# Split query and key parts laid out by dimension then head, spilled part by part, and fetched back in wider transfers

## What is computed

```python
q = heads(hidden_states @ Wq.T + bq)
k = heads(hidden_states @ Wk.T + bk)
v = heads(hidden_states @ Wv.T + bv)
...
scores = jnp.einsum('bhqd,bhkd->bhqk', qx, kx) * scale
return jnp.einsum('bhqk,bhkd->bhqd', jax.nn.softmax(scores, axis=-1), vx)
...
x = x + _layernorm(_L0_attn_ref(_layernorm(x, axis=-1), L0_attn_Wq, ...), axis=-1)
x = x + _layernorm(_L0_ffn_ref(_layernorm(x, axis=-1), ...), axis=-1)
```

## Time and profile before

| | us |
|---|---|
| median of 3 runs (lowest, highest) | 1994.57 (1987.76, 1997.65) |
| the profiled execution | 2002.51 |
| its span, first to last instruction | 2000.7 |
| PE busy / DVE busy / ACT busy / POOL busy | 1591.1 / 1223.5 / 928.4 / 707.2 |

### The profile page before, as it was taken

One profiled execution on the slowest core, in us unless ns is written; L12 is line 12 of the kernel. 1 busy time (PEld: TensorE's weight loads), 2 busy tenths in 40 slices (PEclk: granted clock), 3 DMA queues, 4 the chain that ended last, 5 costly groups with the idle time before them and its releaser, 6 DMA issues. The chain is left out here.

```text
span 2000.7 us, 35686 instructions
## 1 busy us (share of the span) xinstructions
PE 1591.1 (80%) x10365; PEld 1075.6 (54%) x10430; DVE 1223.5 (61%) x3633; ACT 928.4 (46%) x1788; POOL 707.2 (35%) x716
## 2 busy tenths in 40 slices
PE   3878888887887887887888887747999999999800
PEld 2534444444444444444444444536888888888700
DVE  6746765765765765765756755333565656565367
ACT  1045655655655655655656657412333333333234
POOL 1011223413413413314324313432445444444457
PEclk9889999999999998999999999978999999999955
DMA  3453256256265355364365351564665665566477
GB/s 118 78 107 83 55 124 134 82 126 144 72 127 118 89 137 112 81 146 105 90 148 101 82 138 66 167 204 104 139 137 97 142 135 113 123 135 119 49 257 253
DMA packets 185576, 241.78 MB, mean 121 GB/s; under 512 B 24584, under 2 KB 156048, under 8 KB 185296
## 3 DMA queue, kind: packets, MB, share of 16 engines
q1 hardware_dynamic: 158544, 203.58, 40.2%
q0 software_dynamic: 26880, 36.33, 10.9%
HBM read 133.40 MB, written 105.91 MB: 120 GB/s over the span
## 5 line engine op out<-in xcount | busy, mean ns | idle before, releaser
L956 ACT ACTIVATE pexp<-scT 128x512 f32<-128x512 f32 x768 | 440.6, 599 | 366.0 <-PE scT L743 323.7
L1126 DVE TENSOR_REDUCE mx<-work 128x1 f32<-128x320 f32 (+2 forms) x1024 | 493.3, 549 | 60.1 <-PE work L723 57.8
L1600 POOL DMA_INDIRECT y_rows<-rows_add,row_of x144 | 227.0, 1576 | 294.6 <-DMA y_rows<-rows_add,row_of 210.0
L723 PE MATMUL work<-w 126*128 126x320 bf16 (+4 forms) x1280 | 268.0, 302 | 60.3 <-DVE mx L1126 26.6
L743 PE MATMUL scT<-w 128*128 128x192 bf16 (+3 forms) x1472 | 258.8, 274 | 62.8 <-ACT pexp L956 56.9
L1632 PE MATMUL h_ps<-inT,w1c 128*128 128x256 f32 x1152 | 262.1, 381 | 2.4 <-DVE inT L1684 2.4
L1645 PE MATMUL o_ps<-w,hT 128*128 x1152 | 260.4, 379 | 0.0
L1632 PEld LDWEIGHTS h_ps<-inT,w1c 128*128 128x128 f32 x1152 | 219.7, 191 | 33.1 <-issue 3.1
L743 PEld LDWEIGHTS scT<-w 128*128 128x128 bf16 x1536 | 125.6, 98 | 205.4 <-ACT pexp L956 141.6
L1575 ACT ACTIVATE rows_add<-rows_out,row_share 128x257 f32<-128x257 f32 x144 | 65.6, 503 | 355.2 <-DVE rows_out L1700 256.5
L1645 PEld LDWEIGHTS o_ps<-w,hT 128*128 128x128 f32 x1152 | 213.4, 190 | 26.1
(11 more groups left out here) (173 smaller groups left out, 2172.2 us busy)
## 6 DMA issues: line engine op xcount, KB each, us to landing
w<-split_spill SPq DMA_DIRECT2D x384, 128.0 KB, 5.9
split_spill<-split SPq DMA_DIRECT2D x64, 384.0 KB, 4.7
rows_in<-z_rows SPq DMA_DIRECT2D x72, 265.0 KB, 4.7
y_rows<-pre SPq DMA_DIRECT2D x16, 514.0 KB, 6.6
y<-y_rows SPq DMA_DIRECT2D x16, 514.0 KB, 6.1
x_rows<-x SPq DMA_DIRECT2D x16, 512.0 KB, 2.7
abel_rows<-pre SPq DMA_DIRECT2D x16, 512.0 KB, 5.5
abel_in<-abel_rows SPq DMA_DIRECT2D x16, 512.0 KB, 4.5
```

The lines of the kernel that those rows point to most:

```text
L723: ins = nc.tensor.matmul(work[t][:, at:at + hi - lo], tile(qst[par][0:K_SCORE, h, :], t), kst[par][0:K_SCORE, h, lo:hi], start=True, stop= ...
L956: nc.scalar.activation(pexp[:, (q * GROUP + n) % NPB, :], scT[n % 2][:, :], ACT.Exp, scale=DH ** -0.5).then_inc(s_exp, 1)
L1126: nc.vector.reduce_max(mx[:, c:c + 1], work[t][:, 0:n], AX_X).then_inc(w_free[t], 1)
L1600: pool.indirect_dma_start(kept.y_rows, bass.IndirectOffsetOnAxis(ap=row_of[n][:, r:r + 1], axis=0), rows_add[n % 2][:, r, :], None, comput ...
```

## The change

Six edits belong together.

- Queries and keys lie by dimension, then head, within a tile: partition d * 8 + h instead of h * 16 + d. The columns of the query and key weights are permuted for that on DVE: they are loaded to a scratch place (`wqk_raw`, in `ctxT`), and two copies (one for each half of the contraction) put them into `wqkv` in the new order, ahead of the mask rows' copies. The biases are permuted by their DMA. PE's first projection waits for the copies (`s_wqk`).
- One constant load becomes two, so DVE and PE wait for seven constants at the start.
- DRAM holds the spilled tile part by part (`[2, 4, 3, 128, 512]`). Put writes 384 pieces of 1 KB instead of 128 of 3 KB.
- In that layout the 8 heads of one dimension of one part are 8 KB in one piece, and the 16 dimensions and following parts come right behind.
- The six pairs stand in another order (`Q_PART`, `K_PART`), and key tiles hold their parts in reverse (`held`), so that pairs 0 to 2 read three consecutive parts, pairs 3 and 4 of the keys two consecutive parts, pairs 3 and 4 of the queries the same part twice.
- Restack issues three transfers (`GROUPS`) of 48, 32 and 16 partitions instead of six of 16. A stack half is complete after 6 transfers instead of 12.

```diff
-Q_PART = [0, 0, 1, 1, 0, 2]
-K_PART = [0, 1, 0, 1, 2, 0]
+Q_PART = [0, 1, 2, 0, 0, 1]
+K_PART = [2, 1, 0, 1, 0, 0]
+GROUPS = [(0, 3), (3, 5), (5, 6)]
...
+def held(m, part):
+
+    return 2 - part if m % 2 else part
...
+        wqk_raw = ctxT[:, 0:KC, :]
...
-        spill = nc.dram_tensor("split_spill", [2, 4, P, 3, S], BF16, kind="Internal").ap()
+        spill = nc.dram_tensor("split_spill", [2, 4, 3, P, S], BF16, kind="Internal").ap()
...
-            sp.dma_start(wqkv[:, :, :], a["wqkvT"].rearrange("(k p) o -> p k o", p=P)).then_inc(s_const, 16)
-            sp.dma_start(bqk_sb[:, :], a["bqk"]).then_inc(s_const, 16)
+            wqkv_rows = a["wqkvT"].rearrange("(k p) o -> p k o", p=P)
+            sp.dma_start(wqk_raw, wqkv_rows[:, :, 0:2 * D]).then_inc(s_const, 16)
+            sp.dma_start(wqkv[:, :, 2 * D:3 * D], wqkv_rows[:, :, 2 * D:3 * D]).then_inc(s_const, 16)
+            sp.dma_start(bqk_sb[:, :], a["bqk"].rearrange("(h d) m -> d h m", d=DH)).then_inc(s_const, 16)
...
-                sp.dma_start(spill[par, m], split[:, m, :, :]).then_inc(s_spill[m], 16)
+                sp.dma_start(spill[par, m].rearrange("s p c -> p s c"), split[:, m, :, :]).then_inc(s_spill[m], 16)
...
-                for g, part in enumerate(parts):
-                    src = spill[par, m].rearrange("(h d) s c -> d h s c", d=DH)[:, :, part, :]
-                    sp.dma_start(st[par][g * DH:(g + 1) * DH, 8 * half:8 * half + 8, :], src)\
+                for lo, hi in GROUPS:
+                    first, n = held(m, parts[lo]), hi - lo
+                    src = spill[par, m].rearrange("s (d h) c -> s d (h c)", d=DH)
+                    if n > 1 and parts[lo] == parts[lo + 1]:
+                        src = src[first:first + 1].broadcast_to([n, DH, 8 * S])
+                    else:
+                        src = src[first:first + n]
+                    sp.dma_start(st[par][lo * DH:hi * DH, 8 * half:8 * half + 8, :], src)\
                       .then_inc(s_stack[half], 16)
...
+            for k in range(KC):
+                nc.vector.tensor_copy(wqkv[:, k, 0:2 * D].rearrange("p (m d h) -> p m d h", m=4, d=DH),
+                                      wqk_raw[:, k, :].rearrange("p (m h d) -> p m d h", m=4, d=DH)).then_inc(s_wqk, 1)
```

More of the change, by code:

```diff
@@ L312, in front @@
         turn = ps("turn", [P, S])
-        spill = nc.dram_tensor("split_spill", [2, 4, P, 3, S], BF16, kind="Internal").ap()
+        spill = nc.dram_tensor("split_spill", [2, 4, 3, P, S], BF16, kind="Internal").ap()
         s_const = sem("s_const")
+        s_wqk = sem("s_wqk")
         g_load = sem("g_load")
@@ L390, in front @@
         g_t = sem("g_t")
-        N_CONST, N_LOAD, N_INIT = 6, 6, 7
+        N_CONST, N_LOAD, N_INIT = 7, 6, 7
         LOADS = len(RUNS) * 16
@@ L695, in project @@
                     pe.wait_ge(s_xnT, (b + 1) * KC)
+                    if s_is(b, 0):
+                        pe.wait_ge(s_wqk, KC)
                 w = (2 + m) % 4
@@ L717, in max_unit @@
                 if t == 0 and h % 8 == 0:
-                    pe.wait_ge(s_stack[h // 8], (b + 1) * 2 * NGRP * 16)
+                    pe.wait_ge(s_stack[h // 8], (b + 1) * 2 * len(GROUPS) * 16)
                 use(b, t, ("max", h))
@@ L922, in first_part @@
                 wait(act, s_spill[m], b * 16)
-                nc.scalar.activation(split[:, m, 0, :], work[w][:, :], ACT.Identity,
+                nc.scalar.activation(split[:, m, held(m, 0), :], work[w][:, :], ACT.Identity,
                                      bias=bqk_sb[:, m:m + 1]).then_inc(s_part1, 1)
@@ L927, in second_part @@
                 freed(act, b, (2 + m) % 4, "project")
-                nc.scalar.copy(split[:, m, 1, :], resid[:, m % 2, :]).then_inc(s_part2, 1)
+                nc.scalar.copy(split[:, m, held(m, 1), :], resid[:, m % 2, :]).then_inc(s_part2, 1)
             def first_max(b):
@@ L1110, in parts @@
                 nc.vector.scalar_tensor_tensor(out=resid[:, m % 2, :], in0=work[w][:, :],
-                                               scalar=bqk_sb[:, m:m + 1], in1=split[:, m, 0, :],
+                                               scalar=bqk_sb[:, m:m + 1], in1=split[:, m, held(m, 0), :],
                                                op0=ALU.add, op1=ALU.subtract).then_inc(w_free[w], 1)
@@ L1377, in third_part @@
                 pool.wait_ge(s_part2, b * 4 + m + 1)
-                nc.gpsimd.tensor_tensor(split[:, m, 2, :], resid[:, m % 2, :], split[:, m, 1, :],
+                nc.gpsimd.tensor_tensor(split[:, m, held(m, 2), :], resid[:, m % 2, :], split[:, m, held(m, 1), :],
                                         ALU.subtract).then_inc(s_split, 1)
```

## The result

The changed kernel takes 2021.19 us (median of 4 runs, 2017.47 to 2023.61), the kernel before 1995.37 us (4 runs, 1987.76 to 1997.65): ratio 1.0119, 95% interval 1.0094 to 1.0143. The forecast was 1992.4 us in a range of 1983 to 2004. The profiled execution took 2017.47 us with a span of 2015.6 us, 14.9 us more than the profiled one of before. The medians lie 25.8 us apart: the profiled execution of before (2002.51 us) was 7.1 us above its median, and that of the changed kernel is the fastest of its four.

The account below looks back on a forecast made before the run. PE's steady state was held not to be bound by these transfers, only two early waits (5.8 us). Terms: -4.0 for the stacks, +1.8 for the start, together -2.2 us from 1994.6, giving 1992.4 us, range 1983 to 2004.

Parts of the forecast that it names:

- What bounds the kernel: Whole run: restack transfers hold PE up only in steps 1 and 2, 5.8 us; later stacks are early by about 2 us.
- Stacks, the gain: Steps 1 and 2: the half stack lands 2 us earlier, about 230 GB/s, shortening both waits; gain 4.0 us.
- the rival of the two hindered engines: Doubled query part on two slowed DMA engines: half stack 7.8 us later, +93 us, 2087 us; chance 0.08, half past 15 us.
- the unhindered end: Doubled part on two engines at 24.8 GB/s each: half stack lands after 11.1 us, still 2 us earlier.
- That rule of the Trainium skill: Restack's doubled part: engine number is the largest up to 16 dividing both slowest dimensions; cited as speaking against the change.
- The rival's price: Two hindered engines: decides once the half stack takes over 15 us; lateness costs steps 1 and 2 whole, steps 3 to 15 less 2 us.
- Stacks in the loop, 0: Steps 3 to 15: no gain, as the first unit waits for DVE; over 2 us later, each microsecond costs up to 13 us.
- Put, +0.1: Spill to DRAM: 384 pieces instead of 128 add 0.1 us to each put, inside the stack's 2 us; net 0.
- The start, +1.8: Before the first step: one more DMA issue and two copies of 0.68 us each add 1.8 us (1.1 to 3.2).
- Pieces: Restack: 1 KB pieces alone don't explain its low rate, as stores in small pieces reach 373 GB/s; no size given.

Follow-up runs that it names:

- split: Changed kernel with the doubled query part (pairs 3 and 4) fetched by two transfers of 16 partitions instead of one: 2004.84 us against 2003.85 us of the kernel before, 1.0007.
- interleaved: Changed kernel with the dimension outside and the pair inside in the 32-partition transfers, rows ordered to match: 2001.14 us, 1.0009 of the kernel before.
- the padded kernel: Changed kernel with one unused row behind each part in DRAM, so that parts no longer join: 2228.68 us, 1.1121 of the kernel before.
- the second profile of the changed kernel: Changed kernel run again unaltered, beside others on the same chip: 2022.69 us against 2000.41 us of the kernel before, 1.0108.
- the second pair: Dimension-outside, pair-inside layout rerun with the start copies and without them (weights handed over reordered): 2001.01 and 1993.93 us against 1999.09 us of the kernel before.

## Why the prediction was wrong

**What bounds the kernel.** Right. In the two early steps the stack is late, later on it is about 2 us early. In step 7 it came 3.2 us later than before and PE's wait grew from 1.43 to 2.92 us, so 1.7 us of it were covered.

**The step that failed: "Stacks, the gain".** It took a landing 2 us earlier from all sixteen engines at about 230 GB/s. The landing came 3.2 us later instead, because that rate is not what ends a restack. The one transfer in six of a half stack with a leading count of two is. It was the rival of the two hindered engines, rated at 0.08, that decided, and within it the mistake was a size. Each of the two carries 131 + 106 = 237 KB before the half stack is complete. The prediction gave 11.1 us at 24.8 GB/s, the unhindered end, and 20.8 us at 8.8 GB/s. Measured were 16.4 us; less 1.5 us fixed that is 15.9 GB/s. The trace has both sides of this mean: 11 GB/s for each engine while sixteen work at a restack (173 and 177 GB/s), 14.8 GB/s with puts among it, 25 GB/s when two are alone. I held the unhindered rate for likely because two engines hardly press on one receiver. But the other fourteen had work to write for most of that time, the put and the second restack, and the row of 140 GB/s showed the press.

The 230 GB/s was too high as well. Without a small leading count the half stack is used 12.0 us (split) and 11.6 us (interleaved) after the first issue instead of 13.0 us, 1.0 to 1.4 us sooner and not 2. By the prediction's own working that is 188 and 195 GB/s, and the two waits shrank by 2.4 and 2.3 us, not by 4.0. So this term was mis-sized even where its mechanism held.

That rule of the Trainium skill (DMA: Bandwidth & Descriptors, the section on why a DMA increments its semaphore by 16, and its rules for authors) said just this: the slowest dimension sets the number of engines, and a leading broadcast of c copies confines the transfer to at most c. The trace agrees, with a share of 0.13 and 49 GB/s; the padded kernel agrees for leading counts that are no broadcast, with a share of 0.16.

**The rival's price.** It named 15 us as the point from which it decides. With the measured landing its own formula gives 3.2 us in each of steps 1 and 2, 3.2 - 2 = 1.2 us in each of 13 steps, 1.8 us of start, together 23.8 us, so 2018.4 us. The median is 2021.19 us, but that nearness is in good part luck. Steps 1 and 2 waited 6.04 and 6.75 us instead of 3.33 and 2.46 us, 7.0 us more where the formula has 6.4. Of steps 3 to 15 only five waited for the stack, and together they lost 6.7 us where it has 15.6; the start lost 0.4 where it has 1.8. These are 14.1 us of its 23.8, and the rest of the distance between the medians comes from what it didn't count. Why only five of these thirteen steps were late is not shown.

**What the waits don't hold.** The span grew 14.9 us; the waits for stack and `pre` grew 13.7 us, those for ACT fell 4.3 us, the start cost 0.4 us. What remains, some 5 us, may be the clock's: after its longest waits PE goes on at the lower of its two levels. Step 1 after its wait of 6.04 us, and later (PEclk is the last figure but two):

```profile
133.00:136.50 3.50, 3.50 (x31) 1.62 (x32) 1.58 (x3) 0.02 (x1) 0.00 (x0) 0.55 0.85 176
136.50:140.00 3.50, 3.20 (x25) 1.23 (x23) 3.34 (x7) 2.64 (x5) 0.00 (x0) 1.00 0.70 112
```

There three products of a unit take 1.19 us; in the kernel whose wait was 1.62 us they take 0.69 us. A row of before shows it too, 1.20 us after a wait of 3.33 us. The length of the wait alone doesn't decide it: after 2.46 us three products took 1.19 us, after 2.92 us in step 7 of the changed kernel 0.69 us. PE was busy for 1601.6 us in the changed kernel and for 1590.7 us in the interleaved one, with 10429 records each. So a wait's own length was not the whole price, and the prediction counted none of this. The size of this part is a remainder, not a measurement. It is larger elsewhere: in the second profile of the changed kernel the waits for stack and `pre` are 35.6 us, 12.8 us more than in the interleaved kernel on the same chip, and its span of 2020.5 us is 25.5 us longer.

**Stacks in the loop, 0.** Wrong with the landing, though its condition was stated: 2 us of cover, after that each microsecond costs.

**Put, +0.1.** Nothing speaks against it for the put itself (0.9996, 0.9984 to 1.0007, when changed alone), though 0.1 us is far below what the time can show. Missed was what stands behind a slow transfer: put 2 landed after 12.1 us, and the second half's restacks were issued 13.7 us after the first restack instead of 8.6 us (step 7: 559.36 to 573.10; 549.02 to 557.58 before). They have room until head 8.

**The start, +1.8.** Too high. The seventh constant was free, the copies took 0.56 us each instead of 0.68 us, and after the series 0.4 us was left in the first profile. Without the copies and with one constant less the start moved by 1.0 us, and by 1.2 us in the second pair (31.55 to 30.35).

**Pieces.** "Not by themselves" was right, more than was claimed: 8 KB on 16 partitions is no faster than 1 KB. Wider and fewer transfers brought 1.0 to 1.4 us at the stack, and the interleaved kernel shows what the change could give: waits of 3.5 us instead of 5.8 us, and no difference in the time that can be measured.

## What to carry to other kernels

Read the source and target of a transfer by their outermost dimension first: if it counts two or three, only so many DMA engines carry it, and everything queued behind it on them is late. Put a dimension of 16 or more outside, even at the price of another order of rows, or split the transfer. When such a transfer shares its time with others, don't cost it at the rate that an engine has alone: here the two engines came to 15.9 GB/s each over a half stack, against 25 GB/s alone and 11 GB/s while all sixteen worked at a restack.

## What the runs showed of the hardware that was not expected

- Pieces of 8 KB instead of 1 KB to 16 partitions made a restack no faster: 14.35 us from issue to use against 13.0 to 13.2 us.
- Two engines move 49 to 57 GB/s between them when alone, while all sixteen at a restack move 173 to 177 GB/s, 11 GB/s each. So a transfer confined to two is hurt more by its neighbours' traffic than its own bytes would let one think.
- One padding row behind each part, with the same bytes and pieces, took the kernel from 1% to 11% above the one before (2228.68 against 2003.85 us): consecutive parts no longer join to a long outer dimension.
- A microsecond taken from the start came with 6.7 and 7.1 us in two pairs. Its reason stays open, and a difference of 0.3% between two versions of this kernel should not be credited to the edit alone.
